# A fourth slot for the side products, a single bank for the weighted values, and two bursts of value products joined in 15 of 64 heads

## What is computed

```python
h = _layernorm(x, axis=-1) * (1 + ca) + sa
q = (hidden_states @ q_w.T + q_b).reshape(b, s, H, HEAD_DIM)
k = hidden_states @ k_w.T + k_b
v = hidden_states @ v_w.T + v_b
scores = jnp.einsum('bqhd,bkd->bhqk', q, k) / HEAD_DIM ** 0.5
scores = jnp.where(causal[None, None], -jnp.inf, scores)
attn = jax.nn.softmax(scores.astype(jnp.float32), axis=-1).astype(q.dtype)
out = jnp.einsum('bhqk,bkd->bqhd', attn, v).reshape(b, s, H * HEAD_DIM)
return out @ o_w.T + o_b
...
x = x + ga * _L0_attn_ref(h, ...)
h = _layernorm(x, axis=-1) * (1 + cb) + sb
x = x + gb * _L0_ffn_ref(h, ...)
```

## Time and profile before

| | us |
|---|---|
| median of 3 runs | 1965.99 (1965.46 to 1968.29) |
| the profiled execution | 1969.69 |
| its span, from first to last instruction | 1967.7 |
| PE busy in the span | 1893.2 (96%) |
| DVE busy | 1365.5 (69%) |
| ACT busy | 858.1 (44%) |
| POOL busy | 459.7 (23%) |

### The profile page before, as it was taken

How to read it: one execution, slowest core, us unless ns; L and a number is a source line. 1 busy time by engine, 2 the same in 40 slices (tenths; PEclk the granted TensorE clock), 3 DMA queues, 4 the chain that set the end, 5 groups by cost and what they waited for, 6 DMA issues and landing times.

```text
span 1967.7 us, 39650 instructions
## 1 busy us (share of the span) xinstructions
PE 1893.2 (96%) x15040; PEld 1575.5 (80%) x15040; DVE 1365.5 (69%) x3207; ACT 858.1 (44%) x1591; POOL 459.7 (23%) x525
## 2 busy tenths in 40 slices
PE   6999999999999999999999999999999999999998
PEld 3677777777777667667888789999999999999997
DVE  4788686778777666774557797676676776767755
ACT  4367555665556554562223442333323323333221
POOL 2345354535544354361000010010100100101000
PEclk8899999999999999999999999999999999999999
DMA  7432343324333456625448889788788797887884
GB/s 242 120 97 70 96 110 99 98 73 114 102 107 89 141 143 194 216 88 207 139 134 321 334 305 349 285 295 337 284 318 318 290 341 284 296 329 294 331 302 166
DMA packets 118708, 416.19 MB, mean 212 GB/s; under 512 B 26348, under 2 KB 39916, under 8 KB 104312
## 3 DMA queue, kind: packets, MB, share of 16 engines
q1 hardware_dynamic: 106856, 363.27, 54.4%
q10 hardware_dynamic: 11664, 50.40, 6.7%
HBM read 318.16 MB, written 61.10 MB: 193 GB/s over the span
## 4 chain that ended last, share of the span: by engine, by line
PE 47%; DVE 4%; ACT 2%; DMA 2%; issue 1%; SPq 0%; POOL 0%; DVEq 0%; ACTq 0%
PE banks L1811 22%; PE banks L1901 15%; PE banks L1681 8%; DMA upgate_items_dram<-items_ring 1%; PE banks L1777 1%; DVE ln_stats L1255 1%; PE banks L1771 1%; DVE x_normed L1267 0%; DVE y L1380 0%; DMA upgate_raw<-in_w_ug 0%; ACT silu_gate L914 0%; ACT y_split L899 0%; ACT L914 0%; ACT L920 0%; DVE out_sb L1452 0%
## 5 line engine op out<-in xcount | busy, mean ns | idle before, releaser
L1901 PE MATMUL banks<-d_ring,y_split 128*128 128x512 f32 x1536 | 377.5, 392 | 1.9 <-DVE y_split L1400 1.9
L1010 ACT ACTIVATE probs<-banks 128x512 f32<-128x512 f32 x576 | 314.4, 599 | 131.0 <-PE banks L1947 126.7
L1901 PEld LDWEIGHTS banks<-d_ring,y_split 128*128 128x128 f32 x1536 | 281.7, 188 | 56.9 <-DVE y_split L1400 2.1
L1811 PE MATMUL banks<-h_t_split,items_ring 128*128 128x256 f32 x2280 | 321.0, 283 | 1.9 <-DVE both L1357 1.9
L1811 PEld LDWEIGHTS banks<-h_t_split,items_ring 128*128 128x128 f32 x2280 | 299.0, 191 | 13.7 <-ACT h_t L825 4.0
L1735 PE MATMUL banks<-k_stack,q_stacks 96*128 96x512 f32 (+3 forms) x768 | 251.9, 372 | 21.3 <-DVE max_all L1169 7.9
L1947 PE MATMUL banks<-q_stacks,k_stack 98*128 98x512 f32 (+3 forms) x768 | 251.3, 369 | 4.4 <-DMA q_stacks<-neg_max_rows 3.6
L1811 PE MATMUL banks<-input_sums,items_ring 128*128 128x256 f32 x1710 | 236.2, 283 | 0.0
L1111 POOL TENSOR_TENSOR probs<-probs 128x1024 f32<-128x1024 f32 x64 | 153.4, 2398 | 327.1 <-ACT probs L1010 327.1
L1979 PE MATMUL banks<-probs,values 128*32 128x128 f32 (+1 forms) x3328 | 220.5, 320 | 3.1 <-POOL probs L1131 3.1
L1811 PEld LDWEIGHTS banks<-input_sums,items_ring 128*128 128x128 f32 x1710 | 218.9, 192 | 0.0
(11 more groups left out here) (180 smaller groups left out, 2711.5 us busy)
## 6 DMA issues: line engine op xcount, KB each, us to landing
items_ring<-upgate_items_dram SPq DMA_DIRECT2D x94, 1792.0 KB, 7.4
d_ring<-down_split_dram SPq DMA_DIRECT2D x128, 512.0 KB, 8.1
q_stacks<-q_split SPq DMA_DIRECT2D x192, 128.0 KB, 2.7
upgate_raw<-in_w_ug SPq DMA_DIRECT2D x32, 512.0 KB, 4.7
upgate_items_dram<-items_ring ACTq DMA_DIRECT2D x8, 1792.0 KB, 7.6
upgate_items_dram<-items_made ACTq DMA_DIRECT2D x8, 1792.0 KB, 6.8
x<-in_x SPq DMA_DIRECT2D x32, 256.0 KB, 3.0
o_group<-o_and_sums SPq DMA_DIRECT2D x256, 32.0 KB
```

Source lines behind the costliest of these rows:

```text
L1010: nc.scalar.activation(pr[:, probs_slot(H, u), :], score_bank[:, at % SLOTS_SCORE, :], ACT.Exp, scale=SCALE).then_inc(exped, 1)
L1811: last = nc.tensor.matmul(item_bank(g, item), weights[:, a, item, k * P:(k + 1) * P], by_key(item_input(blk, item, m))[:, k, :], start=(k ...
L1901: last = nc.tensor.matmul(acc[:, t, :], ys[s][:, a, t * P:(t + 1) * P], dr[g % D_RING][:, m, :], start=(f == 0 and a + m == 0), stop=(f == ...
```

## The change

The output bank is reduced to one (bank 7) and bank 6 becomes the fourth side slot. The wait of part 0 changes with it: part 0 of head H now waits for the copy of head H - 1. In 15 heads (n = 5, 6, 7, 8 where b > 0, and n = 13 where a sequence follows) part 0 of the head before is moved from the end of that head to unit 4 of this one, directly ahead of part 1. `whole_burst` names these heads. Two bookkeeping edits follow: an early product of the modulation moves from bank 6 to bank 2, and two sets of DMA semaphores of the folding become one set, to make room for the two semaphores of the new slot.

```diff
-PART_BANKS = (6, 7)
+PART_BANKS = (2, 7)
...
+def whole_burst(H, heads):
+
+    b, n = divmod(H, HEADS)
+    return n in OUT_TILES and b > 0 or n == KV_STEP and b + 1 < heads // HEADS
...
-    SLOTS_SCORE, SLOTS_SIDE = 3, 3
-    score_bank, side, obank = banks[:, 0:3, :], banks[:, 3:6, :], banks[:, 6:8, :]
+    SLOTS_SCORE, SLOTS_SIDE = 3, 4
+    score_bank, side, obank = banks[:, 0:3, :], banks[:, 3:7, :], banks[:, 7, :]
...
-    across_in, raw_in, again_in = sem("across_in"), [sem(f"raw_in{n}") for n in range(FOLD_RING)], [sem(f"again_in{n}") for n in range(FOLD_RING)]
+    across_in, fold_in = sem("across_in"), [sem(f"fold_in{n}") for n in range(FOLD_RING)]
...
-                nc.scalar.activation(oraw[:, H % 2, :], obank[:, H % 2, :], ACT.Copy).then_inc(o_copied, 1)
+                nc.scalar.activation(oraw[:, H % 2, :], obank, ACT.Copy).then_inc(o_copied, 1)
...
-                        for r in (1, 2):
+                        for r in range(1, SLOTS_SIDE):
                             side_drained(pe, r)
...
-                    if H >= 2:
-                        pe.wait_ge(o_copied, H - 1)
+                    if H:
+                        pe.wait_ge(o_copied, H)
...
-                    out = obank[row * HD:(row + 1) * HD, H % 2, first * P:(first + len(places)) * P]
+                    out = obank[row * HD:(row + 1) * HD, first * P:(first + len(places)) * P]
...
                     if u == PART_ENDS[0] and H:
+                        if whole_burst(H, ALL):
+                            weigh(H - 1, 0)
                         weigh(H - 1, 1)
-                    if u == (PART_ENDS[1] if H else FIRST_WEIGHED):
+                    if u == (PART_ENDS[1] if H else FIRST_WEIGHED) and not whole_burst(H + 1, ALL):
                         weigh(H, 0)
```

More of the change, by code:

```diff
@@ L1758, in fold_tile @@
                     pe.wait_ge(across_in, 16)
-                    pe.wait_ge(raw_in[i % FOLD_RING], 16 * (i // FOLD_RING + 1))
+                    pe.wait_ge(fold_in[i % FOLD_RING], 16 * (i // FOLD_RING + 1))
                     r = side_slot(key)
@@ L1762, in fold_tile @@
                 else:
-                    pe.wait_ge(again_in[i % FOLD_RING], 16 * (i // FOLD_RING + 1))
+                    pe.wait_ge(fold_in[i % FOLD_RING], 16 * ((FT + i) // FOLD_RING + 1))
                     r = side_slot(key)
```

4 lines of the change are left out of this document (2 added, 2 removed).

## The result

The changed kernel takes 1940.63 us (median of 4 runs, 1939.4 to 1941.8) against 1966.81 us for the kernel before (median of 4): a ratio of 0.9867, 95% interval 0.9849 to 0.9884. So the change is worth some 26 to 29 us where 47.5 were forecast, and 1940.6 lies just above the range of 1900 to 1940.

What follows compares the result with a forecast made beforehand. PE was taken to set the pace, busy 96% of the span. The fourth slot's 43.2 us plus 4.3 for joined bursts made 47.5 us off the median 1966.0, forecasting 1918.5 us, range 1900 to 1940.

Steps and rivals of the forecast that it cites:

- plain heads: Head 34 and 14 like it, transpose to burst: 1.72 us becomes 1.38 with no product held; 0.34 x 14 = 4.8 us.
- n = 1: Among 18 heads where DVE starts late: PE stays behind DVE and gains one step, 0.5 us each, 9.0 in all.
- the output tiles: Heads n = 6 to 8: maxima product after the tile no longer waits for DVE's reading; 0.47 x 9 = 4.2 us.
- The seam: Between the two joined parts of a burst: taken to cost 0.11 us, possibly nothing or 0.29.
- The joined bursts: In 15 heads one way in and one way out of a burst go: 0.29 us each, 4.3 us in all.
- Rival 3: Joined bursts hold ACT: exponentials 3 and 4 outlast part 1, unit 6 waits; 16 us over 15 heads, 1935 us; chance 0.05.
- Heads 58 to 61: Heads with foldings at the end of attention: estimated slot gain of 3.0 us, within 12.0 for heads 46 to 61.
- Ends of n = 10 to 12: Row transposes at the ends of n = 9 to 12 start earlier with the fourth slot: 0.31 x 12 = 3.7 us.
- the heads with keys: Three heads where projections wait for the split and a maxima product for ACT's second pass: 1.85 x 3 = 5.6 us.
- Rival 2: Only PE's idle time counts, late products stay late behind DVE: gain 22 to 31 us, 1935 to 1944; chance 0.18.
- Rival 1: Every slot wait goes, DVE never being next: 64 us, with the bursts 68, giving 1898 us; chance 0.12.
- rival 4: Part 0 stalls on the single output bank's copy, in 48 heads with part 0 in unit 8: 2012 us; chance 0.05.

Runs made afterwards that it cites:

- e2: Kernel before with a single output bank alone, three side slots and two bursts in every head: 1971.01 us, ratio 1.0011.
- e1: Changed kernel without the joined bursts, four side slots and one output bank kept: 1936.41 us, ratio 0.9828.
- e8: Changed kernel with four fold buffers instead of two and joined bursts at n = 6 alone: 1932.34 us, ratio 0.9819.
- e12: Changed kernel with four fold buffers, joins at n = 6 alone, and GpSimd's second sum waiting for VectorE's row split in n = 9 to 12: 1927.54 us, ratio 0.9787.
- e6: Changed kernel without joined bursts, with four buffers instead of two for the folded rows: 1933.82 us, ratio 0.9819.
- e9: Changed kernel with ScalarE's square root replaced by Identity and the exponential behind it left out (computation incomplete): 1942.13 us, ratio 0.9864.
- e10: Changed kernel without joined bursts, with the square root and the exponential behind it taken out (computation incomplete): 1934.97 us, ratio 0.9824.

## Why the prediction was wrong

**Right, by its own steps.** That a slot wait costs its wait and 0.10 more, and that a fourth slot gives one step of the reader and not every wait: plain heads 0.34 forecast, 0.30 to 0.40 measured; n = 1 0.50 and 0.48 to 0.50; the output tiles 0.47 and, without joins, 0.41 to 0.48 in heads 22 to 24 and 38 to 40; n = 5 1.10 and 1.03, 1.07, 1.13; n = 13 1.81 and 1.71 to 1.73; n = 9 0.81 and 0.79; heads 47, 48 and 50, 0.67 and 0.74. The seam: the first product of part 1 starts 0.095 us after the last of part 0, for 0.11. The single bank at nothing (e2).

**Wrong, in order of size.**

1. *The joined bursts, +4.3 forecast, -6.6 measured* (e1). The step that failed is "DVE loses the burst at the end of the head before ...; in n = 5 and 13 the query projection covers it, in 6 to 8 the output tile". I compared the burst with the two reductions of its own head, and not with the whole of what VectorE has queued up to the next slot that PE wants. In n = 5 that is statistics, output group, reciprocal, output split and query split, 8.29 us from the last maxima product for 7.01 of PE's work. In n = 13 it is the split of the rows that the projection itself reads. By kinds, after the saving: n = 5 cost 0.7 to 1.3 us in head 21 and 0.14 in head 53, n = 13 0.67 each, n = 6 to 8 0.20 and 0.99 for three. The saving itself was sized right (0.25 to 0.31 for 0.29, e8 and e12). Rival 3 looked for the loss on ScalarE behind part 0; it was on VectorE ahead of it.
2. *Heads 58 to 61, 3.0 forecast, and 2 in head 57.* The slot gave 2.30 in head 57, and head 58 gave back 2.75, in e1: about 1.2 behind a transfer, as in the profiles with that wait alone, and some 1.5 in a half-clock stretch, for which the forecast had no term and which is not in every execution. The step had followed slots alone; the ring of two buffers was already the releaser of one wait of 1.1 us in the profile before, which I had not read, since it did not reach PE. Measured with four buffers: 3.55 for heads 57 to 61 (e6).
3. *Ends of n = 10 to 12, 0.31 x 9 = 2.8 forecast, nothing measured.* These heads gained 0.48, the term for the late start alone. The transposes did come earlier; the split after them then met GpSimd's sum in full (1.78 us for 1.47 before), so VectorE started the next head later by what PE had saved. In e12 they gained 1.03.
4. *Small*: head 18 lost 0.55 us where 0.34 was to be gained, in every kernel with four slots. It is the same collision of VectorE and GpSimd: at the head's start an instruction of VectorE on 8 columns, with two inputs in SBUF, takes 1.16 us behind GpSimd's sum, where it takes 0.17 in the kernel before.

```profile
263.53 1.16 DVE L1188 SCALAR_TENSOR_TENSOR neg_max<-max_all,neg_max 128x8 fp32r<-128x8 f32 x1 [0.21 <-DVE neg_max L1187]
263.37 1.29 POOL L1119 TENSOR_TENSOR probs<-probs 128x512 f32<-128x512 f32 x1
```

Head 30 lost 0.43; the cause stays open. Heads 20 and 36 wait for a transfer of queries (the entry with DMA above, 1.7 us at most), differently in every execution, and head 36 often holds a half-clock stretch besides. Heads 6 and 7 were forecast at 0.50 each and gained 1.09 and 0.01, right only as a sum. Two slips in the sum are small too: "head 34, and 14 like it" are fifteen heads and fourteen were counted, and the heads with keys were taken at 1.85 where their parts give 1.81.

Together, by the profiled executions: 10.9 us on the joins and 9.4 on the slots (43.2 forecast, 33.8 in e1, of which some 4.8 in heads 57 to 61, clock included, and 2.8 to 3.1 in n = 10 to 12) make the 20.3 between 47.5 and 27.2.

**The rivals.** Rival 2 (only idle time counts) would have given 1935 to 1944 and holds the measured time, but not its reason: by its own test plain heads would gain under 0.2 us, and they gain 0.38. Rival 1 is out by its own test (heads n = 1 gain 0.50 and not 1.4), rival 4 by e2. The range was too narrow on that side: it allowed 10 us either way for "stretches priced by one example", and both large misses lay in places for which no stretch had been followed, behind the edit and not at it.

## What to carry to other kernels

Before a piece of PE work is moved away, follow the other engines' queues from there to the next thing of theirs that PE wants, and compare the whole of it with what PE has left to do: here 2 us of burst covered a chain of 8.3 that no view of waits named, because it was covered. When an engine gets earlier, look at what it then collides with: a transfer that takes the same time as ever, and a neighbour on a shared port. An instruction whose longest duration is twice its median for the same shape held, in all four places followed here, a wait that no entry shows, and in one of them a single wait on the other engine removed it (e12: 9 x 0.55 = 4.9 us). Before one head of one profile is called a gain or a loss, look whether a half-clock stretch lies in it, and look at the same head in a second profile: here 1.5 of the 3.6 us between two kernels in head 58 were such a stretch.

## What the runs showed of the hardware

- A VectorE subtraction of two 128x512 tiles in SBUF takes 0.69 us, and 1.78 when it starts 0.07 us after a GpSimd sum of 1.32 us; one of 64 columns 0.22 and 1.31. With the start moved by a wait all 32 took 0.69.
- A transfer of 512 KB to HBM landed in 3.0 us at the median and in 6.9 where loads of 1024 and 512 KB ran beside it.
- Taking two table loads of 1.28 us on ScalarE out brought nothing (e9, e10): VectorE's next instruction started 0.75 us earlier in its queue and took 0.75 us longer behind a GpSimd addition.
- The block reaches small instructions: one of VectorE on 8 columns took 1.16 us for 0.17 behind a GpSimd sum (head 18).
- TensorE ran at 1.2 GHz (granted clock 0.50) for stretches of some 3.4 us within attention, two in the profile of the kernel before (its mean of 1.00 in the earlier trace rows is rounded) and three in that of the changed one; the two shown began 1.9 and 1.3 us after PE had waited 1.74 and 1.43 us. One of them in head 58 cost 1.3 to 1.6 us, by the profiles with and without it.
